# Turns of tiles alone: a tile's loads of weights go out together, after the adding transfers issued last

## What is computed

```python
logits = xn2 @ w_gate                              # 8 experts
top_vals, top_idx = jax.lax.top_k(logits, 2)
gates = jax.nn.softmax(top_vals, axis=-1)          # two experts for each token
def body(acc, p):                                  # for each expert
    w1, bb1, w2, bb2, g = p
    h = jax.nn.gelu(xn2 @ w1 + bb1, approximate=False)
    return (acc + g[:, None] * (h @ w2 + bb2), None)
```

## Time and profile before

| | |
|---|---|
| median of 3 runs | 2596.96 us (2594.35 to 2597.08) |
| profiled execution | 2601.49 us, of it the span 2599.6 |
| mean granted TensorE clock | 0.935 |
| busy share of the span: PE, PEld, DVE, ACT, POOL | 92%, 71%, 64%, 45%, 40% |
| transfers: WF, WB, XtR, B2t | 96 of each over the span |

### The profile page before, as it was taken

One profiled execution on the slowest core, in us unless ns is written; L12 is line 12 of the kernel. 1 busy time (PEld: TensorE's weight loads), 2 busy tenths in 40 slices (PEclk: granted clock), 3 DMA queues, 4 the chain that ended last, 5 costly groups with the idle time before them and its releaser, 6 DMA issues. The chain is left out here.

```text
span 2599.6 us, 64053 instructions
## 1 busy us (share of the span) xinstructions
PE 2382.5 (92%) x19496; PEld 1836.3 (71%) x19496; DVE 1658.9 (64%) x4146; ACT 1158.6 (45%) x2240; POOL 1042.2 (40%) x1196
## 2 busy tenths in 40 slices
PE   5589999999999999999999999999999988999886
PEld 4456666666666666677777777777777667888886
DVE  3558888888888888867767776777667731111111
ACT  2234443444433444355555565555555643333332
POOL 2103333333333333244444444444444454555555
PEclk8679999999999998899999999999999999999998
DMA  7432222321223222544344455544534356878774
GB/s 136 150 40 33 33 34 46 45 32 33 34 41 50 32 32 36 135 91 97 102 110 98 106 114 118 113 96 106 117 89 104 95 158 197 219 209 226 203 214 122
DMA packets 250837, 262.98 MB, mean 101 GB/s; under 512 B 35477, under 2 KB 230489, under 8 KB 250777
## 3 DMA queue, kind: packets, MB, share of 16 engines
q1 hardware_dynamic: 213912, 229.95, 37.2%
q0 software_dynamic: 36864, 32.27, 7.2%
HBM read 212.21 MB, written 52.83 MB: 102 GB/s over the span
## 5 line engine op out<-in xcount | busy, mean ns | idle before, releaser
L1347 DVE TENSOR_REDUCE MX<-PS 108x2 f32<-108x648 f32 x576 | 456.0, 824 | 45.6 <-PE PS L1769 40.9
L1042 ACT ACTIVATE pool<-PS 108x648 f32<-108x648 f32 x576 | 387.4, 714 | 216.5 <-PE PS L1792 186.4
L890 POOL DMA_INDIRECT out<-big,tokn x192 | 304.2, 1584 | 436.2 <-DVE big L1497 232.2
L1648 PE MATMUL PS<-WB,big 128*128 128x192 f32 x2304 | 406.3, 332 | 2.5 <-ACT big L1071 2.5
L1071 ACT ACTIVATE big<-PS,WF 128x256 f32<-128x256 f32 x576 | 242.2, 473 | 371.6 <-PE PS L1648 369.9
L1648 PE MATMUL PS<-XE,WF 128*128 128x256 f16 x2880 | 366.4, 279 | 35.3 <-DMA WF<-w1p 28.2
L1648 PEld LDWEIGHTS PS<-WB,big 128*128 128x128 f32 x2304 | 375.6, 192 | 27.4 <-issue 18.5
L1648 PEld LDWEIGHTS PS<-XE,WF 128*128 128x128 f16 x2880 | 277.9, 100 | 91.2 <-issue 33.5
L867 POOL DMA_INDIRECT xbuf<-XR,DST x192 | 190.5, 992 | 242.5 <-issue 197.8
L1497 DVE SCALAR_TENSOR_TENSOR big<-PS,grow,GB 128x192 f32<-128x192 f32 x192 | 71.3, 413 | 273.5 <-POOL GB L878 144.2
L1803 PE MATMUL PS<-pool,Vp 108*32 108x324 f32 x2304 | 217.5, 520 | 0.0
(11 more groups left out here) (197 smaller groups left out, 4104.1 us busy)
## 6 DMA issues: line engine op xcount, KB each, us to landing
WF<-w1p SPq DMA_DIRECT2D x96, 771.5 KB, 5.1
WB<-in_L_ffn_W SPq DMA_DIRECT2D x96, 576.0 KB, 4.7
ximg<-in_x SPq DMA_DIRECT2D x96, 196.0 KB, 5.3
XtR<-xbuf SPq DMA_DIRECT2D x96, 196.0 KB, 2.5
ximg<-in_x SPq DMA_DIRECT2D x96, 195.1 KB, 8.7
B2t<-in_L_ffn_b SPq DMA_DIRECT2D x96, 96.0 KB, 5.3
out<-R SPq DMA_DIRECT2D x32, 243.0 KB
w1p<-WF SPq DMA_DIRECT2D x8, 768.0 KB, 4.0
```

Source lines behind the costliest of these rows:

```text
L890: nc.gpsimd.indirect_dma_start(rows_out, bass.IndirectOffsetOnAxis(ap=tokn[:, i, s_:s_ + 1], axis=0), Yt[:, i, s_, :], None, bounds_check= ...
L1042: nc.scalar.activation(Pr[:, at:at + 2, :], pair(("st", p))[0:TP, :, 0:T], ACT.Exp, scale=SCALE2).then_inc(S["ex"], 1)
L1347: nc.vector.tensor_reduce(MX[:, qt, g, 64 * jj:64 * jj + 64:32], pair(("s", p))[0:TP, :, 0:T], AX.X, ALU.max).then_inc(S["mx"], 1)
L1648: last = nc.tensor.matmul(out_ap, lhsT, rhs, start=(i == 0), stop=(i == len(products) - 1))
```

## The change

`TILE_STEPS` gets another order for `lr`, `lu` and `ld`, and on SyncE each `ld` of these turns first waits on the semaphore of the adding transfers that were issued before this tile's own. The order of the steps of PE, ScalarE, VectorE and GpSimd stays as it is, and so do all waits in them.

```diff
 TILE_STEPS = [
-    ("gm", 0), ("gb", 0), ("lr", 0), ("W1", 0, 0), ("ge", 0, 0), ("X", 1), ("xe", 1), ("gm", 1), ("gb", 1), ("lr", 1),
-    ("W1", 0, 1), ("ge", 0, 1), ("W1", 0, 2), ("ge", 0, 2), ("lu", 0), ("W1", 1, 0), ("ge", 1, 0), ("X", 2),
-    ("xe", 2), ("W1", 1, 1), ("ge", 1, 1), ("W2", 0, 0), ("W2", 0, 1), ("yv", 0), ("ld", 0), ("ad", 0), ("gm", 2),
-    ("gb", 2), ("lr", 2), ("W1", 1, 2), ("ge", 1, 2), ("lu", 1), ("W1", 2, 0), ("ge", 2, 0), ("X", 0), ("xe", 0),
-    ("W1", 2, 1), ("ge", 2, 1), ("W1", 2, 2), ("ge", 2, 2), ("lu", 2), ("W2", 1, 0), ("W2", 1, 1), ("yv", 1),
-    ("ld", 1), ("ad", 1), ("W2", 2, 0), ("W2", 2, 1), ("yv", 2), ("ld", 2), ("ad", 2),
+    ("gm", 0), ("gb", 0), ("W1", 0, 0), ("ge", 0, 0), ("X", 1), ("xe", 1), ("gm", 1), ("lr", 0), ("lr", 1), ("ld", 0),
+    ("lu", 0), ("gb", 1), ("W1", 0, 1), ("ge", 0, 1), ("W1", 0, 2), ("ge", 0, 2), ("W1", 1, 0), ("ge", 1, 0),
+    ("X", 2), ("xe", 2), ("W1", 1, 1), ("ge", 1, 1), ("W2", 0, 0), ("W2", 0, 1), ("yv", 0), ("ad", 0), ("gm", 2),
+    ("lr", 2), ("ld", 1), ("lu", 1), ("gb", 2), ("W1", 1, 2), ("ge", 1, 2), ("W1", 2, 0), ("ge", 2, 0), ("X", 0),
+    ("xe", 0), ("W1", 2, 1), ("ge", 2, 1), ("W1", 2, 2), ("ge", 2, 2), ("W2", 1, 0), ("W2", 1, 1), ("yv", 1),
+    ("ad", 1), ("W2", 2, 0), ("W2", 2, 1), ("yv", 2), ("ad", 2), ("ld", 2), ("lu", 2),
 ]
```

```diff
+            def landed(m, i):
+                if i:
+                    sp.wait_ge(S[f"ad{i - 1}"], due(f"ad{i - 1}", m, 32))
+                else:
+                    sp.wait_ge(S["ad2"], due("ad2", m - 1, 32))
+                apart(sp)
+
...
                     elif step[0] == "ld" and not turn.last:
+                        if turn.plan is TILES:
+                            landed(item, step[1])
                         load_down(item + 1, step[1])
```

## The result

| | before | after |
|---|---|---|
| median of the runs, us | 2595.65 (2589.12 to 2597.08) | 2689.91 (2688.84 to 2692.23) |
| ratio | 1 | 1.0369, 95% interval 1.035 to 1.0389 |
| profiled execution, us | 2601.49 | 2690.78, span 2689.0 |

A forecast was written before the change was run, and what follows sets the result against it. The loop of adding-transfer pairs, each issued after the last one's landing, was taken to bound the tile turns; 47 intervals growing from 8.60 to 9.20 us add 28 us, giving 2625 us beside the median, range 2578 to 2645.

The forecast's parts named there:

- What bounds the kernel: Turns of tiles alone: paced by adding-transfer pairs, each landing releasing the next, 47 intervals of 8.60 us.
- When the loads go: In all three intervals, ld at +0.2 and lu at +2.4 us from the pair's first transfer, ahead of its second.
- The price of an interval: Time from pair to pair with ld and lu issued at its start: 9.2 us taken, bounds 8.54 and 9.9.
- About half of it I take as hidden, because a lone WF starts slowly.: In the interval, ld replacing lr adds 476 KB, 1.2 us; about half hidden beside WF's slow start, leaving 0.66.
- The upper end, 9.9: Interval with everything in a row: 1.0 + 1.0 + 6.83 engine time + 1.1 us; +61 us in all.
- The sum: Over the tile turns: 47 x (9.20 - 8.60) = +28 us, 2625 beside the median.
- Idle time: TensorE in the tile turns: from about 32 us to about 60, without becoming the bound.
- rival 4: Tile turns: TensorE starves if WF lands over 2 us later than worked out; one microsecond beyond gives 2641; chance 0.06.
- Rival 1: Tile turns: adding transfers slip past the loads, TensorE's work sets turns of 23.8 to 24.8 us; 2566 to 2581; chance 0.22.
- Rival 2: Tile turns: tile 0's interval gives back what the others pay, mean 8.5 to 8.7 us; 2592 to 2602; chance 0.10.
- Rival 3: SyncE's loads: waits change nothing in time order, as o_full holds ld anyway; same interval as forecast, counted within its 0.62.
- the lower row: Lower end of the interval: tile 2's, with lr and lu at its start, mean 8.54 us; -3 us in all.

The follow-up runs named there:

- experiment 5: Kernel after, with half of TensorE's second product (W2) left out in the turns of tiles alone: 2689.40 us, ratio 1.0355.
- experiment 7: Kernel after, each ld waiting for its own pair's issue, signalled by a GpSimd memset, instead of the previous pair's landing: 2702.89 us, ratio 1.0407.
- experiment 10: Kernel before with the three added waits (old order), ld2 and its wait moved behind the next turn's lr0: 2565.42 us, ratio 0.9899.
- experiment 1: Kernel after with the new load order but without the added waits in front of each ld: 2614.82 us, ratio 1.0066.
- experiment 4: Kernel before with another load order and a counter that GpSimd raises behind each pair's issue and SyncE waits for: 2600.91 us, ratio 1.0014.

## Why the prediction came out as it did

**What bounds the kernel: right.** The loop from a pair's issue over its landing to the next pair's issue paced the tile turns before and after; experiment 5 took work from TensorE and gained nothing.

**When the loads go: right.** WB at A+0.34 and WF at A+2.47, where +0.2 and +2.4 were forecast, in all three intervals, and the intervals became equal. The prediction had both loads ahead of the second transfer. The packets show more: WB stands ahead of the first as well, whose first 11 packets move between 2424 and 2425 us, over 3.3 us after its issue began.

**The price of an interval: wrong, and this is the term that failed.** The value taken was 8.54 + 0.66 = 9.2 us; measured are 10.51. Two steps of it failed.
- *"About half of it I take as hidden, because a lone WF starts slowly."* The step is ld in the place of lr, put at 0.66 us; it measured 10.51 - 8.54 = 2.0. First the rate. The 476 KB were priced at 383 GB/s, which is WF's in its second microsecond. WB and B2t start slowly themselves: 98, 268 and 292 GB/s, 3 us for their 0.65 MB, where lr's 196 KB took one (2312 to 2313, 199 GB/s). So the packets of the pair begin nearly 2 us later, not 1.2. Then the half that was hidden. WF does start slowly, and alone: the DMA view of the kernel before has only loads from 2314 to 2315. But ahead of that come the packets of the first adding transfer with WF's first, from 2313 to 2314, as they do in the kernel after from 2425 to 2427. WF's start follows the end of the load before it in both kernels, and the 2.0 us leave nothing of ld hidden there. Those two windows of the kernel before, 2313 to 2314 and 2314 to 2315:

```profile
q1 hardware_dynamic: 39, 0.10, 61.7%
q0 software_dynamic: 127, 0.08, 57.3%
...
q1 hardware_dynamic: 39, 0.24, 74.9%
```

- *The upper end, 9.9, was no upper end.* Built up again from the rows for the interval of 10.64 us: from the landing before to the pair 0.83 and to ld 0.34, so 1.17 (1.0 in the prediction). To the first packets 1.0, as forecast. The packets run from 2422 to just under 2430, about 8 us, where the mean engine time of 6.83 had been put; the landing shows at 2430.49, about 0.5 us behind them, where 1.1 had been put. That engine time held (0.66 x 477/45.4 intervals = 6.9, and the shares of the eight stretches add up to 7.0), but sixteen engines aren't busy all the while: in the first microsecond they are at 0.81, in the last a quarter busy. So 0.2 and 1.2 us more and 0.6 less, 0.7 in all. The row of VectorE that shows the landing, against the earlier trace rows:

```profile
2430.49 0.17 DVE L1514 CAST tokn<-XtR 128x2 uint32<-128x2 f32 x1 [9.06 <-DMA out<-big,tokn]
```

**The sum.** With 10.51 in the place of 9.20 it reads 47 x 1.91 = 90 us, for 89.3 between the profiled executions and 94 between the medians. The count, the base and the sign stood; the size of one term was off, by a factor of three, and the range hung on the same term. A bound that takes the engines as busy from the first packet to the last is no upper end.

**TensorE: right in kind, low in size.** Idle time was forecast at about 60 us; it is 103.5. WF lands 7.0 us after its issue (5.6 to 7.8), not 5.1 as in the earlier trace rows. That is the edge of the "over 7 us" of rival 4. It did not come to bind, since the longer interval also gave it more room: the pair may go two intervals after the landing, 21.0 us now, where the load and the work need 1.1 + 2.2 + 7.0 + 7 + 0.8 = 18.1. Experiment 5 shows that room; experiment 7 shows the rival once the pairs are short.

**The clock.** TensorE stood idle from 2424 us, and in the stretches above its granted clock falls from 1.00 to 0.55 and 0.50 (the lower level, 1.2 GHz) from 2427 on. Over the tile turns it is 0.90, before 0.96. It costs nothing here, by experiment 5.

**The rivals.** Rival 1, in which the adding transfers slip through, is refuted for this order: at 10.5 us an interval they did not. But its turn of about 24 us came with another order, experiment 10. The prediction took the Trainium skill's turn-taking between queues, packet by packet ("DMA: Bandwidth & Descriptors", section "Queues, rings and completion order"), to mean that a load issued ahead would hardly hold an adding transfer back. That reading fails here: from 2422 to 2425 there are 865 packets of loads and 11 of the adding transfer, though the first transfer's issue had ended at 2422.28. The rule itself isn't refuted: the section lets an engine drain up to 64 descriptors of one queue before it switches, and if each packet of the profile is one of these, 865 over 16 engines are 54 each. The rule of the same section that an increment lands only behind every earlier write agrees with the landings, 6.7 us with the loads ahead (the kernel after) and 3.6 with them behind (experiment 7). The prediction named that rule, with the interval at its upper end, and still stayed nearer to the lower row. Rival 2, evened out, had the shape right (three equal intervals) and the level wrong. Rival 3 was counted with the forecast, and nothing speaks for it: the loads left at other times than before, and experiment 1 shows how much of the loss is gone without the waits.

## What to carry to other kernels

Where a transfer's landing paces a loop, ask for every load what it stands in front of at the moment when it is let go, and price it by its own packets, with their slow start, and not by the best rate of another load; a wait is harmless or harmful by what is queued behind it (here the same three waits gave -17 us with WF issued before them and, with WF behind them, turned the order's +20 into +94). A wait that keeps two large loads apart can pay; one that gathers them at the start of the transfer that binds does not. And split a slow microsecond by queue before explaining it: the share says that engines are busy, not with whom.

## What the runs showed of the hardware that was not expected

- Loads issued before or during the issue of an adding transfer went almost wholly ahead of it: 865 packets against 11 in 3 us. Against the 6.3 us estimated for a full pair with nothing in front, a load of 672 KB ahead made the interval 1.1 to 1.2 us longer, WB and WF together 4.2 us.
- The adding transfers keep the engines busy at a low rate by themselves. In the microsecond from 2330 of experiment 7 no load moves, and 114 of their packets, 0.08 MB, make a share of 0.84 at 84 GB/s. Beside WF in the kernel after it is 129 and 173 GB/s at shares of 1.30 and 0.78; WF alone has 372 at 0.89. Half of WF less is worth 2.0 us an interval, at 190 KB/us. The row of experiment 7:

```profile
q0 software_dynamic: 114, 0.08, 83.7%
```

- GpSimd's increment of a counter behind two adding transfers let SyncE go before the second had begun (experiment 4); with a memset behind them, and a wait of its own ahead of it, SyncE went 2.9 us after the second transfer's start (experiment 7).
- What wasn't tried: an order in which WF goes behind one pair and WB behind another with room for both. Experiment 10 comes near to it and leaves 14 us in 362 in which TensorE idles.
